# A feed-forward layer with a sine: angle and turns made by ScalarE straight from PSUM, rounding in one VectorE operation, the sine added by TensorE through a diagonal

## The chip, the cores and the metric

The kernel runs on one core of a Trainium2 chip, as one launch. The metric is the device time of that launch in microseconds (us). A core has a matrix engine (TensorE, PE in the profile, with its weight loads as PEld), a vector engine (VectorE, DVE), a scalar engine for activations (ScalarE, ACT), a general engine (GpSimd, POOL) and a queue engine (SyncE, SP). Each works through its own list of instructions in order and waits for the others by semaphores.

## The reference

Four layers, each an attention-like part and a feed-forward part, are applied to 2 x 1024 tokens of width 128 with a layer norm ahead of each. The change is in the feed-forward part of the first layer:

```python
imag = w_imag * jnp.sin(theta + hidden * 0.1)
quantum_phase = jnp.cos(theta) * w_real + jnp.sin(theta) * w_imag
return hidden + quantum_phase * imag * 0.1
...
hidden = jnp.einsum('bsd,df->bsf', x, W1) + b1
q = _quantum_transform(hidden, quantum_phases, quantum_weights_real, quantum_weights_imag)
act = jax.nn.relu(q)
return jnp.einsum('bsf,fd->bsd', act, W2) + b2
```

Width 128 goes to 512 hidden features and back. `theta`, `w_real` and `w_imag` have one value for each hidden feature, so everything that multiplies the sine is one coefficient per feature, `coef`.

## The kernel before

The program is a row of stages, one after the other on the same core; each allocates its own buffers and semaphores, and all engines meet at a barrier at its end. Nothing of a later stage is loaded ahead. The stage of the change is `l0_ffn`, whose buffers are named l0f_ in the profile. Its input is `xnT`, the normalised tokens with features on the 128 partitions and 2048 tokens along the rest; its result is added to `x`.

The work is cut into 16 items `n` = (g, c): four groups `g` of 512 tokens times four chunks `c` of 128 hidden features. For one item the kernel before does this:

- TensorE: a 128x512 matmul of `w1` and `xnT` into one of two PSUM buffers `hid` (L1014).
- ScalarE, `keep` (L932): hidden plus `b1` out of PSUM into `h`.
- VectorE, `angle`: the argument 0.1 h + theta (L973), then `turns_removed`, which takes whole turns out of it, since the sine is wanted on a bounded argument: multiply and add the constant `ROUND` (L882), subtract it again (L883), three multiply-and-subtract operations with the parts of two pi (L885), a clamp (L886).
- ScalarE, `sine` (L936), then VectorE, `combine` (L979): h + coef * sine, then ScalarE, `relu` (L943), into `a`.
- TensorE, `down` (L1007): after the four chunks of a group, 16 matmuls of 128x128, four for each chunk, into `outp`; then VectorE, `add` (L986), adds `outp` to `x`.

`h` and `y` have three buffers each, `hid` and `outp` two. A float32 matmul stands in the trace as two records, and has two weight loads. The order of work on each engine is written out by hand: VectorE does `angle(n)`, then `combine(n - 1)`, and at n = 5, 9 and 13 `add` of the group before. TensorE does `down(g - 1)` behind the matmul of item 4g + 1, but it runs ahead of the other engines, and so takes each chunk as soon as its `relu` is done. Every operation of `angle` waits for the one ahead of it to be done (`step.then_wait`), as it reads that one's result. At the stage's start VectorE works out `coef` on 128x4 tiles, and GpSimd adds the output bias to `x` (L918).

Of the kernel before, what the change touches and what calls it, by code (L numbers as in the profile page):

```python
# [5 lines left out]
ALU = mybir.AluOpType  # L6
ACT = mybir.ActivationFunctionType
# [6 lines left out]
P = 128  # L14
# [860 lines left out]
TWO_PI_PARTS = (6.28125, 0.0019350051879882812, 3.0199159819e-07)  # L875
ROUND = 1.5 * 2.0 ** 23
PI_IN = 3.1415925


def turns_removed(dve, step, y, m):  # L880

    step.then_wait(dve, dve.tensor_scalar(m, y, 0.15915494309189535, ROUND, ALU.mult, ALU.add))  # L882
    step.then_wait(dve, dve.tensor_scalar(m, m, ROUND, None, ALU.subtract))  # L883
    for part in TWO_PI_PARTS:
        step.then_wait(dve, dve.scalar_tensor_tensor(y, m, -part, y, ALU.mult, ALU.add))  # L885
    return dve.tensor_scalar(y, y, PI_IN, -PI_IN, ALU.min, ALU.max)  # L886


def l0_ffn(nc, d, x, xnT):

    F = d["f0_w1"].shape[1]
    FC = F // P
    with ExitStack() as ctx:
        sb, pb, sem = scope(nc, ctx, "l0f")
        w1, w2 = sb("w1", [P, F]), sb("w2", [P, FC, P])
        vec = sb("vec", [P, 4, FC])
        b2 = sb("b2", [P, P])
        coef, cosr, sinr, room = (sb(n, [P, FC]) for n in ("coef", "cosr", "sinr", "room"))
        h, y, m = sb("h", [P, 3, 512]), sb("y", [P, 3, 512]), sb("m", [P, 512])
        a = sb("a", [P, 2, FC, 512])  # L900
        hid = [pb(f"hid{n}", [P, 512]) for n in range(2)]
        outp = [pb(f"outp{n}", [P, 4, P]) for n in range(2)]
        w_in, bias_added = sem("w_in"), sem("bias_added")
        hid_ready, hid_kept, y_ready, sine_done = sem("hid_ready"), sem("hid_kept"), sem("y_ready"), sem("sine_done")
        q_ready, act_ready, out_ready, out_kept = sem("q_ready"), sem("act_ready"), sem("out_ready"), sem("out_kept")
        dve_step, angle_ready, trig_ready = sem("dve_step"), sem("angle_ready"), sem("trig_ready")
        items = [(g, c) for g in range(4) for c in range(FC)]
        block = ctx.enter_context(nc.Block(no_gpsimd_drain=True))

        @block.sync  # L910
        def _(sp):
            for dst, src in ((w1, d["f0_w1"]), (vec, d["f0_vec"]), (w2, d["f0_w2"]), (b2, d["f0_b2"].partition_broadcast(P))):
                sp.dma_start(dst[:], src).then_inc(w_in, 16)

        @block.gpsimd
        def _(pool):
            pool.wait_ge(w_in, 64)
            pool.tensor_tensor(x[:, :, :], x[:, :, :], b2[:, :].unsqueeze(1).broadcast_to([P, TT, P]),  # L918
                               ALU.add).then_inc(bias_added, 1)

        @block.scalar
        def _(act):
            act.wait_ge(angle_ready, 1)
            act.activation(sinr[:, :], vec[:, 1, :], ACT.Sin).then_inc(trig_ready, 1)
            act.activation(cosr[:, :], vec[:, 1, :], ACT.Sin, scale=0.5).then_inc(trig_ready, 1)

            def keep(n):
                g, c = items[n]
                act.wait_ge(hid_ready, n + 1)
                if n >= 3:  # L930
                    act.wait_ge(act_ready, n - 2)
                act.activation(h[:, n % 3, :], hid[n % 2][:, :], ACT.Identity, bias=vec[:, 0, c:c + 1]).then_inc(hid_kept, 1)  # L932

            def sine(n):
                act.wait_ge(y_ready, n + 1)
                act.activation(y[:, n % 3, :], y[:, n % 3, :], ACT.Sin).then_inc(sine_done, 1)  # L936

            def relu(n):
                g, c = items[n]
                act.wait_ge(q_ready, n + 1)  # L940
                if g >= 2:
                    act.wait_ge(out_ready, g - 1)
                act.activation(a[:, g % 2, c, :], h[:, n % 3, :], ACT.Relu).then_inc(act_ready, 1)  # L943

            keep(0)
            for n in range(len(items)):
                if n + 1 < len(items):
                    keep(n + 1)
                sine(n)
                if n >= 1:  # L950
                    relu(n - 1)
            relu(len(items) - 1)

        @block.vector
        def _(dve):
            step = Count(dve_step)
            dve.wait_ge(w_in, 64)
            turns_removed(dve, step, vec[:, 1, :], room[:, :]).then_inc(angle_ready, 1)
            dve.wait_ge(trig_ready, 2)

            step.then_wait(dve, dve.tensor_tensor(cosr[:, :], cosr[:, :], cosr[:, :], ALU.mult))
            step.then_wait(dve, dve.tensor_scalar(cosr[:, :], cosr[:, :], -2.0, 1.0, ALU.mult, ALU.add))
            step.then_wait(dve, dve.tensor_tensor(cosr[:, :], cosr[:, :], vec[:, 2, :], ALU.mult))
            step.then_wait(dve, dve.tensor_tensor(coef[:, :], sinr[:, :], vec[:, 3, :], ALU.mult))
            step.then_wait(dve, dve.tensor_tensor(coef[:, :], coef[:, :], cosr[:, :], ALU.add))
            step.then_wait(dve, dve.tensor_tensor(coef[:, :], coef[:, :], vec[:, 3, :], ALU.mult))
            step.then_wait(dve, dve.tensor_scalar(coef[:, :], coef[:, :], 0.1, None, ALU.mult))

            def angle(n):
                g, c = items[n]  # L970
                dve.wait_ge(hid_kept, n + 1)
                s = y[:, n % 3, :]
                step.then_wait(dve, dve.tensor_scalar(s, h[:, n % 3, :], 0.1, vec[:, 1, c:c + 1], ALU.mult, ALU.add))  # L973
                turns_removed(dve, step, s, m[:, :]).then_inc(y_ready, 1)

            def combine(n):
                g, c = items[n]
                dve.wait_ge(sine_done, n + 1)
                dve.scalar_tensor_tensor(h[:, n % 3, :], y[:, n % 3, :], coef[:, c:c + 1], h[:, n % 3, :],  # L979
                                         ALU.mult, ALU.add).then_inc(q_ready, 1)  # L980

            def add(g):
                dve.wait_ge(out_ready, g + 1)
                dve.wait_ge(bias_added, 1)
                s = x[:, 4 * g:4 * g + 4, :]
                dve.tensor_tensor(s, outp[g % 2][:, :, :], s, ALU.add).then_inc(out_kept, 1)  # L986

            for n in range(len(items)):
                angle(n)
                if n >= 1:  # L990
                    combine(n - 1)
                if n % FC == 1 and n > FC:
                    add(n // FC - 1)
            combine(len(items) - 1)
            add(3)

        @block.tensor
        def _(pe):
            pe.wait_ge(w_in, 64)

            def down(g):
                if g >= 2:
                    pe.wait_ge(out_kept, g - 1)
                for c in range(FC):
                    pe.wait_ge(act_ready, FC * g + c + 1)
                    for t in range(4):
                        mm = pe.matmul(outp[g % 2][:, t, :], a[:, g % 2, c, t * P:(t + 1) * P], w2[:, c, :],  # L1007
                                       start=(c == 0 and t == 0), stop=(c == FC - 1), skip_group_check=True)
                mm.then_inc(out_ready, 1)

            for n, (g, c) in enumerate(items):
                if n >= 2:
                    pe.wait_ge(hid_kept, n - 1)
                pe.matmul(hid[n % 2][:, :], w1[:, c * P:(c + 1) * P], xnT[:, g * 512:(g + 1) * 512],  # L1014
                          start=True, stop=True).then_inc(hid_ready, 1)
                if c == 1 and g >= 1:
                    down(g - 1)
            down(3)
def l1_attention(nc, d, x, xnT, ident):

# [1606 lines left out]
def program(nc, d, out, upto=99, start=0):  # L2627
    with ExitStack() as ctx:
        sb, pb, sem = scope(nc, ctx, "main")
        x = sb("x", [P, TT, P])  # L2630
        xnT = sb("xnT", [P, TOK])
        ident = sb("ident", [P, P])
# [12 lines left out]
        def layer(n, name, f, **k):  # L2645
            if start <= n < upto:
                prenorm(nc, "n" + name, x, xnT, ident, **k)
                f()

        layer(0, "0", lambda: l0_attention(nc, d, x, xnT, ident, None), rounds=2, gamma=gin[:, :])  # L2650
        layer(1, "1", lambda: l0_ffn(nc, d, x, xnT))
        layer(2, "2", lambda: l1_attention(nc, d, x, xnT, ident))

        def l1_ffn():
# [51 lines left out]
```

## Time and profile before

| | |
|---|---|
| median of 3 runs | 2371.45 us (2366.53 to 2375.58) |
| the profiled execution's own time | 2371.62 us |
| its span | 2369.9 us |
| the stage, first matmul to end of last add | 1321.58 to 1409.32 us, 87.7 us |

The profile is of one execution. The span runs from its first to its last recorded instruction. Times of day below are microseconds from the span's start. The busy share of an engine counts the instructions' own time; the granted clock (PEclk) is a share of full speed, 0.50 being 1.2 GHz and 1.00 being 2.4 GHz, averaged over a stretch.

### The profile page before, as it was taken

How to read it: one execution, taken by the hardware profiler on the slowest of the kernel's cores; microseconds unless marked ns; L12 is line 12 of the kernel's file. 1: busy time of each engine (PE TensorE's matmuls, PEld its weight loads, DVE VectorE, ACT ScalarE, POOL GpSimd, SP SyncE). 2: the span in 40 equal slices, each digit the busy share in tenths (PEclk: the TensorE clock that was granted, in tenths of full speed). 3: DMA queues.
4: the chain of work that ended last, by engine and by line, in shares of the span. 5: the costliest groups of instructions: out<-in, count | busy, mean ns of one | idle time of the engine just before them, and what ended most of it. 6: DMA issues, size and time to landing. Idle time of an engine off the chain costs nothing. (4 is left out here: it accounts for less than half of the span.)

```text
span 2369.9 us, 25752 instructions
## 1 busy us (share of the span) xinstructions
PE 1798.6 (76%) x8561; PEld 1103.2 (47%) x8561; DVE 1164.2 (49%) x2590; ACT 778.7 (33%) x1139; POOL 789.6 (33%) x618
## 2 busy tenths in 40 slices
PE   3999999999989999999997448795422853767647
PEld 1555555555555555555556234663422521222337
DVE  5434434344344442443433883345760356999814
ACT  1343334333423344333431332132101135545312
POOL 0433343333413443334331001000104301889533
PEclk8898989989899899898998667797656965899858
DMA  2101110011101100111000000000131101222051
GB/s 56 23 6 23 22 22 18 4 22 22 23 1 23 23 18 4 22 22 22 18 0 1 11 0 6 1 18 12 48 121 57 54 13 38 80 80 71 20 141 62
DMA packets 52733, 72.67 MB, mean 31 GB/s; under 512 B 10320, under 2 KB 36072, under 8 KB 52384
## 3 DMA queue, kind: packets, MB, share of 16 engines
q1 hardware_dynamic: 49744, 65.69, 10.3%
q0 software_dynamic: 2912, 6.02, 0.7%
q8 instruction: 40, 0.66, 0.1%
q14 instruction: 37, 0.30, 0.0%
HBM read 42.75 MB, written 12.15 MB: 23 GB/s over the span
## 5 line engine op out<-in xcount | busy, mean ns | idle before, releaser
L763 DVE TENSOR_REDUCE l0a_mx<-l0a_ring 128x1 fp32r<-128x128 f32 (+7 forms) x256 | 182.4, 751 | 175.7 <-PE l0a_ring L513 175.5
L771 DVE SCALAR_TENSOR_TENSOR l0a_scrap<-l0a_ring,main_ident 128x128 f32<-128x128 f32 x256 | 74.5, 291 | 348.6 <-PE l0a_ring L541 250.9
L354 POOL TENSOR_TENSOR l0a_acc<-l0a_acc,l0a_E 128x768 f32<-128x768 f32 (+2 forms) x192 | 212.5, 1132 | 69.1 <-ACT l0a_E L424 68.2
L354 POOL TENSOR_TENSOR l0a_acc<-l0a_E 128x896 f32<-128x896 f32 x32 | 66.1, 2085 | 454.2 <-ACT l0a_E L424 454.2
L540 PE MATMUL l0a_ring<-l0a_Q,l0a_K 128*128 128x512 f32 (+3 forms) x384 | 174.8, 458 | 47.7 <-ACT l0a_E L424 47.4
L424 ACT ACTIVATE l0a_E<-l0a_ring 128x1024 f32<-128x1024 f32 (+7 forms) x256 | 161.4, 650 | 130.3 <-DVE l0a_scrap L771 127.2
L2370 PE MATMUL mx_ysum<-mx_hst,main_ident 128*128 128x512 f32 x256 | 141.4, 687 | 46.1 <-POOL mx_hst L2458 40.6
L2471 POOL TENSOR_TENSOR mx_dBu<-mx_XI,mx_BB 128x1024 f32<-128x1024 f32 x64 | 137.5, 2176 | 91.9 <-DVE mx_XI L2534 91.9
L511 PE MATMUL l0a_ring<-l0a_K,l0a_Q 64*128 64x512 f32 (+3 forms) x384 | 140.5, 419 | 25.9 <-DVE l0a_mx L763 21.0
L553 PE MATMUL l0a_agg<-l0a_E,l0a_VH 128*64 128x512 f32 (+3 forms) x768 | 154.6, 510 | 0.2 <-ACT l0a_E L424 0.2
L553 PE MATMUL l0a_agg<-l0a_E,l0a_F 128*64 128x512 f32 (+3 forms) x768 | 148.5, 502 | 0.0
L541 PE MATMUL l0a_ring<-l0a_Q,l0a_K 65*128 65x512 f32 (+3 forms) x384 | 146.1, 380 | 0.0
L540 PEld LDWEIGHTS l0a_ring<-l0a_Q,l0a_K 128*128 128x128 f32 x384 | 84.0, 219 | 128.7 <-ACT l0a_E L424 102.0
L2443 ACT ACTIVATE mx_dA<-mx_DT,mx_A 128x512 f32<-128x512 f32 x128 | 88.0, 690 | 98.6 <-DVE mx_hst L2551 98.5
L2370 PEld LDWEIGHTS mx_ysum<-mx_hst,main_ident 128*128 128x128 f32 x256 | 53.6, 217 | 117.1 <-POOL mx_hst L2458 59.6
L511 PEld LDWEIGHTS l0a_ring<-l0a_K,l0a_Q 64*128 64x128 f32 x384 | 64.3, 193 | 83.4 <-DVE l0a_mx L763 60.2
L162 PE MATMUL n_turned<-main_ident,n_xn 128*128 128x128 f32 x96 | 25.8, 456 | 89.7 <-DVE n_xn L132 89.7
L491 PE MATMUL l0a_ring<-l0a_wp,main_xnT 128*128 128x256 f32 x256 | 85.5, 506 | 3.1 <-DVE l0a_mx L763 3.1
L2551 DVE TENSOR_TENSOR_SCAN mx_hst<-mx_dA,mx_hst,mx_dBu 128x512 f32<-128x512 f32 x64 | 82.1, 1283 | 7.6 <-DVE mx_hst L2551 0.5
L601 PEld LDWEIGHTS l0a_prod<-l0a_gnn,l0a_UT 128*128 128x128 f32 x512 | 77.9, 229 | 15.2 <-issue 13.0
L601 PE MATMUL l0a_prod<-l0a_gnn,l0a_UT 128*128 128x128 f32 x512 | 83.8, 317 | 0.7 <-ACT l0a_UT L451 0.7
L541 PEld LDWEIGHTS l0a_ring<-l0a_Q,l0a_K 65*128 65x128 f32 x384 | 83.0, 216 | 0.8
(467 smaller groups left out, 3613.2 us busy)
## 6 DMA issues: line engine op xcount, KB each, us to landing
mx_BB<-mx_brows SPq DMA_DIRECT2D x32, 512.0 KB, 3.6
l0a_K<-l0a_K SPq DMA_DIRECT2D x32, 256.0 KB, 3.7
l0a_Q<-l0a_Q SPq DMA_DIRECT2D x32, 256.0 KB, 4.4
me_W<-in_f_w SPq DMA_DIRECT2D x16, 256.0 KB, 9.2
l0a_wp<-in_wqkv SPq DMA_DIRECT2D x16, 192.0 KB, 2.3
moe_Wg<-in_f_wg SPq DMA_DIRECT2D x8, 256.0 KB
moe_Wu<-in_f_wu SPq DMA_DIRECT2D x8, 256.0 KB
moe_Wd<-in_f_wd SPq DMA_DIRECT2D x8, 256.0 KB
```

The costliest lines, as they stand in the source:

```text
L354: pool.tensor_tensor(dst, src, E[:, h, ecol[jt]:ecol[jt] + w], ALU.add).then_inc(acc_done, 1)
L424: act.activation(E[:, h, ecol[jt]:ecol[jt] + w], ring[h][:, 0:w], ACT.Exp).then_inc(exp_done, 1)
L491: mm = pe.matmul(ring[c][:, t * 2 * P:(t + 1) * 2 * P], xnT[:, tok:tok + P], wp[:, 2 * P:4 * P], start=True, stop=True)
L511: pe.matmul(ring[h][:, c0:c1], Q1[0:DH, h, it * P:(it + 1) * P], K1[0:DH, h, c0:c1], start=True, stop=c1 < w)
L540: pe.matmul(out, K1[:, h, keys], Q1[:, h, at], start=True, stop=False, skip_group_check=True)
L541: mm = pe.matmul(out, K2[:, h, keys], Q2[:, h, at], start=False, stop=c0 > 0, skip_group_check=True)
L553: mm = pe.matmul(agg[c][cols, lo - 512 * c:512], feats[:, jt, cols], E[:, h, at + lo:at + hi], start=(jt == 0), stop=(jt == 4 * c + 3 and ...
L601: mm = pe.matmul(prod[:, t * P:(t + 1) * P], UT[:, at:at + P], gnn[l][:, :], start=True, stop=True)
L763: dve.tensor_reduce(mx[:, h, it:it + 1], ring[h][:, 0:(it + 1) * P], AX_X, ALU.max).then_inc(max_done, 1)
L2370: mm = pe.matmul(ysum[h][:, c * 512:(c + 1) * 512], ident[:, :], hst[:, k % DEEP, c * 512:(c + 1) * 512], start=(n == 0), stop=(n == NS - ...
L2443: act.activation(dA[:, c * 512:(c + 1) * 512], DT[:, h, b * SEQ + c * 512:b * SEQ + (c + 1) * 512], ACT.Exp, scale=A[:, h, n:n + 1]).then_ ...
L2471: pool.tensor_tensor(dBu[:, k % DEEP, :], du_of(h, b), BB[:, q % 3, :], ALU.mult).then_inc(dBu_ready, 1)
```

## The change

ScalarE reads each matmul's result from PSUM twice (`angle`): once as turns, hidden/(10 * 2 pi) + `start`, into `m`, and once as the angle, 0.1 hidden + `phase`, into `y`. `phase` and `start` are worked out once on 128x4 tiles. VectorE (`reduce`) rounds `m` by one operation that adds and subtracts `ROUND`, then does the three subtractions and the clamp as before. `hidden` is not kept apart any more: TensorE adds coef * sine to the hidden values in their PSUM buffer, by a 128x512 matmul with the diagonal matrix `diag` (`add_sine`), and `relu` reads the sum from PSUM and adds `b1`. `combine` is gone. `hid` now has four buffers instead of two, each held from its first matmul until its `relu`; `y` and `m` have four each. `diag` is made by four VectorE operations. `add` on VectorE stands behind the whole of `reduce` of item 4g + 2, and `down(g - 1)` on TensorE behind `add_sine(4g + 1)` and the hidden matmul of item 4g + 4.

```diff
--- before.py
+++ after.py
@@ -886,7 +886,11 @@
     return dve.tensor_scalar(y, y, PI_IN, -PI_IN, ALU.min, ALU.max)
 
 
-def l0_ffn(nc, d, x, xnT):
+TURN = 0.15915494309189535
+HIDS, WORKS = 4, 4
+
+
+def l0_ffn(nc, d, x, xnT, ident):
 
     F = d["f0_w1"].shape[1]
     FC = F // P
@@ -896,15 +900,19 @@
         vec = sb("vec", [P, 4, FC])
         b2 = sb("b2", [P, P])
         coef, cosr, sinr, room = (sb(n, [P, FC]) for n in ("coef", "cosr", "sinr", "room"))
-        h, y, m = sb("h", [P, 3, 512]), sb("y", [P, 3, 512]), sb("m", [P, 512])
+        phase, start = sb("phase", [P, FC]), sb("start", [P, FC])
+        diag = sb("diag", [P, FC, P])
+        y, m = sb("y", [P, WORKS, 512]), sb("m", [P, WORKS, 512])
         a = sb("a", [P, 2, FC, 512])
-        hid = [pb(f"hid{n}", [P, 512]) for n in range(2)]
+        hid = [pb(f"hid{n}", [P, 512]) for n in range(HIDS)]
         outp = [pb(f"outp{n}", [P, 4, P]) for n in range(2)]
         w_in, bias_added = sem("w_in"), sem("bias_added")
...
         dve_step, angle_ready, trig_ready = sem("dve_step"), sem("angle_ready"), sem("trig_ready")
         items = [(g, c) for g in range(4) for c in range(FC)]
+        N = len(items)
         block = ctx.enter_context(nc.Block(no_gpsimd_drain=True))
 
         @block.sync
@@ -923,41 +931,61 @@
             act.wait_ge(angle_ready, 1)
             act.activation(sinr[:, :], vec[:, 1, :], ACT.Sin).then_inc(trig_ready, 1)
             act.activation(cosr[:, :], vec[:, 1, :], ACT.Sin, scale=0.5).then_inc(trig_ready, 1)
-
-            def keep(n):
+            act.wait_ge(angle_ready, 2)
+
+            def angle(n):
                 g, c = items[n]
                 act.wait_ge(hid_ready, n + 1)
-                if n >= 3:
-                    act.wait_ge(act_ready, n - 2)
-                act.activation(h[:, n % 3, :], hid[n % 2][:, :], ACT.Identity, bias=vec[:, 0, c:c + 1]).then_inc(hid_kept, 1)
+                if n >= WORKS:
+                    act.wait_ge(sum_ready, n - WORKS + 1)
+                w = n % WORKS
+                act.activation(m[:, w, :], hid[n % HIDS][:, :], ACT.Identity, bias=start[:, c:c + 1],
+                               scale=0.1 * TURN).then_inc(turns_kept, 1)
+                act.activation(y[:, w, :], hid[n % HIDS][:, :], ACT.Identity, bias=phase[:, c:c + 1],
+                               scale=0.1).then_inc(angle_kept, 1)
 
             def sine(n):
                 act.wait_ge(y_ready, n + 1)
-                act.activation(y[:, n % 3, :], y[:, n % 3, :], ACT.Sin).then_inc(sine_done, 1)
+                act.activation(y[:, n % WORKS, :], y[:, n % WORKS, :], ACT.Sin).then_inc(sine_done, 1)
 
             def relu(n):
                 g, c = items[n]
-                act.wait_ge(q_ready, n + 1)
+                act.wait_ge(sum_ready, n + 1)
                 if g >= 2:
                     act.wait_ge(out_ready, g - 1)
-                act.activation(a[:, g % 2, c, :], h[:, n % 3, :], ACT.Relu).then_inc(act_ready, 1)
-
-            keep(0)
-            for n in range(len(items)):
-                if n + 1 < len(items):
-                    keep(n + 1)
+                act.activation(a[:, g % 2, c, :], hid[n % HIDS][:, :], ACT.Relu, bias=vec[:, 0, c:c + 1]).then_inc(act_ready, 1)
+
+            angle(0)
+            angle(1)
+            for n in range(N):
                 sine(n)
+                if n + 2 < N:
+                    angle(n + 2)
                 if n >= 1:
                     relu(n - 1)
-            relu(len(items) - 1)
+            relu(N - 1)
 
         @block.vector
         def _(dve):
             step = Count(dve_step)
             dve.wait_ge(w_in, 64)
             turns_removed(dve, step, vec[:, 1, :], room[:, :]).then_inc(angle_ready, 1)
+            dve.wait_ge(angle_ready, 1)
+            step.then_wait(dve, dve.scalar_tensor_tensor(phase[:, :], vec[:, 0, :], 0.1, vec[:, 1, :], ALU.mult, ALU.add))
+            dve.tensor_scalar(start[:, :], phase[:, :], TURN, None, ALU.mult).then_inc(angle_ready, 1)
+
+            def reduce(n):
+                w = n % WORKS
+                k, s = m[:, w, :], y[:, w, :]
+                dve.wait_ge(turns_kept, n + 1)
+                step.then_wait(dve, dve.tensor_scalar(k, k, ROUND, ROUND, ALU.add, ALU.subtract))
+                dve.wait_ge(angle_kept, n + 1)
+                for part in TWO_PI_PARTS:
+                    step.then_wait(dve, dve.scalar_tensor_tensor(s, k, -part, s, ALU.mult, ALU.add))
+                dve.tensor_scalar(s, s, PI_IN, -PI_IN, ALU.min, ALU.max).then_inc(y_ready, 1)
+
+            reduce(0)
             dve.wait_ge(trig_ready, 2)
-
...
-
-            def angle(n):
-                g, c = items[n]
-                dve.wait_ge(hid_kept, n + 1)
-                s = y[:, n % 3, :]
-                step.then_wait(dve, dve.tensor_scalar(s, h[:, n % 3, :], 0.1, vec[:, 1, c:c + 1], ALU.mult, ALU.add))
-                turns_removed(dve, step, s, m[:, :]).then_inc(y_ready, 1)
-
-            def combine(n):
-                g, c = items[n]
-                dve.wait_ge(sine_done, n + 1)
-                dve.scalar_tensor_tensor(h[:, n % 3, :], y[:, n % 3, :], coef[:, c:c + 1], h[:, n % 3, :],
-                                         ALU.mult, ALU.add).then_inc(q_ready, 1)
+            for c in range(FC):
+                dve.tensor_scalar(diag[:, c, :], ident[:, :], coef[:, c:c + 1], None, ALU.mult).then_inc(coef_ready, 1)
 
             def add(g):
                 dve.wait_ge(out_ready, g + 1)
@@ -985,13 +1002,10 @@
                 s = x[:, 4 * g:4 * g + 4, :]
                 dve.tensor_tensor(s, outp[g % 2][:, :, :], s, ALU.add).then_inc(out_kept, 1)
 
-            for n in range(len(items)):
-                angle(n)
-                if n >= 1:
-                    combine(n - 1)
-                if n % FC == 1 and n > FC:
+            for n in range(1, N):
+                reduce(n)
+                if n % FC == 2 and n > FC:
                     add(n // FC - 1)
-            combine(len(items) - 1)
             add(3)
 
         @block.tensor
@@ -1008,13 +1022,30 @@
                                        start=(c == 0 and t == 0), stop=(c == FC - 1), skip_group_check=True)
                 mm.then_inc(out_ready, 1)
 
-            for n, (g, c) in enumerate(items):
-                if n >= 2:
-                    pe.wait_ge(hid_kept, n - 1)
-                pe.matmul(hid[n % 2][:, :], w1[:, c * P:(c + 1) * P], xnT[:, g * 512:(g + 1) * 512],
-                          start=True, stop=True).then_inc(hid_ready, 1)
-                if c == 1 and g >= 1:
-                    down(g - 1)
+            def hidden(n):
+                g, c = items[n]
+                if n >= HIDS:
+                    pe.wait_ge(act_ready, n - HIDS + 1)
+                pe.matmul(hid[n % HIDS][:, :], w1[:, c * P:(c + 1) * P], xnT[:, g * 512:(g + 1) * 512],
+                          start=True, stop=False, skip_group_check=True).then_inc(hid_ready, 1)
+
+            def add_sine(n):
+                g, c = items[n]
+                pe.wait_ge(sine_done, n + 1)
+                pe.wait_ge(angle_kept, n + 1)
+                if n == 0:
+                    pe.wait_ge(coef_ready, FC)
+                pe.matmul(hid[n % HIDS][:, :], diag[:, c, :], y[:, n % WORKS, :], start=False, stop=True,
+                          skip_group_check=True).then_inc(sum_ready, 1)
+
+            for n in range(3):
+                hidden(n)
+            for n in range(N):
+                add_sine(n)
+                if n + 3 < N:
+                    hidden(n + 3)
+                if n % FC == 1 and n > FC:
+                    down(n // FC - 1)
             down(3)
 def l1_attention(nc, d, x, xnT, ident):
```

The two places where the order counts follow. On VectorE, around the first `add`, items 5 to 7 before (L979 is `combine`, L973 to L886 are `angle`, L986 is `add`):

```order
L886 TENSOR_SCALAR l0f_y<-l0f_y 128x512
L979 SCALAR_TENSOR_TENSOR l0f_h<-l0f_y,l0f_coef,l0f_h 128x512
L986 TENSOR_TENSOR main_x<-l0f_outp,main_x 128x512
L973 TENSOR_SCALAR l0f_y<-l0f_h,l0f_vec 128x512
L882 TENSOR_SCALAR l0f_m<-l0f_y 128x512
L883 TENSOR_SCALAR l0f_m<-l0f_m 128x512
L885 SCALAR_TENSOR_TENSOR l0f_y<-l0f_m,l0f_y 128x512 x3
```

The same place now (L981 rounds, L984 subtracts, L985 clamps, L1003 is `add`):

```order
L981 TENSOR_SCALAR l0f_m<-l0f_m 128x512
L984 SCALAR_TENSOR_TENSOR l0f_y<-l0f_m,l0f_y 128x512 x3
L985 TENSOR_SCALAR l0f_y<-l0f_y 128x512
L1003 TENSOR_TENSOR main_x<-l0f_outp,main_x 128x512
L981 TENSOR_SCALAR l0f_m<-l0f_m 128x512
L984 SCALAR_TENSOR_TENSOR l0f_y<-l0f_m,l0f_y 128x512 x3
```

`add(0)` has gone from behind item 5's angle to behind item 6's, and `reduce(7)` stands behind it.

On TensorE, around the first `down`, before (L1014 is the hidden matmul of items 3 to 7, L1007 is `down`):

```order
L1014 MATMUL l0f_hid1<-main_xnT,l0f_w1 128x512
L1014 MATMUL l0f_hid0<-main_xnT,l0f_w1 128x512
L1014 MATMUL l0f_hid1<-main_xnT,l0f_w1 128x512
L1007 MATMUL l0f_outp0<-l0f_w2,l0f_a 128x128 x16
L1014 MATMUL l0f_hid0<-main_xnT,l0f_w1 128x512
L1014 MATMUL l0f_hid1<-main_xnT,l0f_w1 128x512
```

The same place now (L1029 is the hidden matmul of items 7, 8 and 9, L1038 is `add_sine` of items 5, 6 and 7, L1021 is `down(0)`):

```order
L1029 MATMUL l0f_hid3<-main_xnT,l0f_w1 128x512
L1038 MATMUL l0f_hid1<-l0f_y,l0f_diag 128x512
L1029 MATMUL l0f_hid0<-main_xnT,l0f_w1 128x512
L1021 MATMUL l0f_outp0<-l0f_w2,l0f_a 128x128 x16
L1038 MATMUL l0f_hid2<-l0f_y,l0f_diag 128x512
L1029 MATMUL l0f_hid1<-main_xnT,l0f_w1 128x512
L1038 MATMUL l0f_hid3<-l0f_y,l0f_diag 128x512
```

`down(0)` has moved behind the hidden matmul of item 8, which waits for `relu(4)`, and the sums of items 6 and 7 stand behind it.

## Rows read from the trace of the kernel before

**Rows 1.** The page's head, and the first row of the chain that ended last:

```profile
span 2369.9 us, 25752 instructions
...
2274.58 0.06 issue
```

**Rows 2.** Busy us of PE, PEld, DVE, ACT, POOL, granted clock, DMA share, GB/s:

```profile
1320.00:1410.00 90.00, 49.62 (x160) 31.34 (x160) 79.84 (x145) 30.46 (x50) 4.50 (x1) 0.67 0.00 1
1352.00:1354.00 2.00, 2.00 (x9) 2.00 (x10) 1.88 (x4) 0.00 (x0) 0.00 (x0) 0.50 0.00 0
1354.00:1356.00 2.00, 2.00 (x4) 0.81 (x3) 1.95 (x4) 0.25 (x1) 0.00 (x0) 0.52 0.00 0
1356.00:1366.00 10.00, 4.79 (x22) 2.61 (x20) 9.55 (x18) 4.90 (x9) 0.00 (x0) 1.00 0.00 1
1366.00:1368.00 2.00, 1.47 (x7) 1.48 (x8) 1.86 (x5) 1.16 (x2) 0.00 (x0) 0.54 0.00 0
1840.00:1880.00 40.00, 40.00 (x214) 29.16 (x213) 15.03 (x36) 9.61 (x22) 12.44 (x13) 1.00 0.07 22
2070.00:2090.00 20.00, 11.19 (x28) 4.28 (x28) 18.85 (x17) 9.61 (x14) 20.00 (x10) 0.99 0.17 56
```

**Rows 3.** Timeline of one item: start us, us, engine, line, operation [idle before <-releaser]:

```profile
1384.28 0.74 DVE L979 SCALAR_TENSOR_TENSOR l0f_h<-l0f_y,l0f_coef,l0f_h 128x512 f32<-128x512 f32 x1
1384.94 0.48 DVE L973 TENSOR_SCALAR l0f_y<-l0f_h,l0f_vec 128x512 f32<-128x512 f32 x1
1385.45 0.43 DVE L882 TENSOR_SCALAR l0f_m<-l0f_y 128x512 f32<-128x512 f32 x1
1385.91 0.43 DVE L883 TENSOR_SCALAR l0f_m<-l0f_m 128x512 f32<-128x512 f32 x1
1386.38 2.14 DVE L885 SCALAR_TENSOR_TENSOR l0f_y<-l0f_m,l0f_y 128x512 f32<-128x512 f32 x3
1388.55 0.43 DVE L886 TENSOR_SCALAR l0f_y<-l0f_y 128x512 f32<-128x512 f32 x1
1388.90 0.74 DVE L979 SCALAR_TENSOR_TENSOR l0f_h<-l0f_y,l0f_coef,l0f_h 128x512 f32<-128x512 f32 x1
1389.01 0.63 ACT L936 ACTIVATE l0f_y<-l0f_y 128x512 f32<-128x512 f32 x1 [2.55 <-DVE l0f_y L886]
```

**Rows 4.** Timeline, ScalarE and matmuls, at both levels of the clock:

```profile
1321.58 3.76 PE L1014 MATMUL l0f_hid<-main_xnT,l0f_w 128*128 128x512 f32 x4 [6.64 <-DMA l0f_b<-in_f_b]
...
1327.16 1.25 ACT L932 ACTIVATE l0f_h<-l0f_hid,l0f_vec 128x512 f32<-128x512 f32 x2
...
1334.03 2.08 PE L1014 MATMUL l0f_hid<-main_xnT,l0f_w 128*128 128x512 f32 x2 [3.04 <-ACT l0f_h L932]
...
1358.31 1.12 PE L1014 MATMUL l0f_hid<-main_xnT,l0f_w 128*128 128x512 f32 x2 [0.69 <-ACT l0f_h L932]
...
1404.82 3.78 PE L1007 MATMUL l0f_outp<-l0f_w,l0f_a 128*128 128x128 f32 x16 [2.60 <-ACT l0f_a L943]
...
1833.86 2.97 PE L1875 MATMUL e_outp<-moe_Wd,e_a 128*128 128x128 f32 x24
```

**Rows 5.** Groups by line, stage: busy us, mean ns | idle before, releaser:

```profile
L932 ACT ACTIVATE l0f_h<-l0f_hid,l0f_vec 128x512 f32<-128x512 f32 x16 | 10.8, 684 | 12.3 <-PE l0f_hid L1014 11.3
```

**Rows 6.** Timeline of the stage's ends, the adds, and a VectorE scaling:

```profile
1298.16 2.14 DVE L865 TENSOR_SCALAR l0a_Y<-l0a_Y,l0a_l0o_mv,l0a_l0o_rstd 128x128 f32<-128x128 f32 x8
...
1326.76 0.17 DVE L886 TENSOR_SCALAR l0f_vec<-l0f_vec 128x4 f32<-128x4 f32 x1
...
1355.75 0.68 DVE L986 TENSOR_TENSOR main_x<-l0f_outp,main_x 128x512 f32<-128x512 f32 x1
...
1394.18 0.68 DVE L986 TENSOR_TENSOR main_x<-l0f_outp,main_x 128x512 f32<-128x512 f32 x1
1394.78 0.48 DVE L973 TENSOR_SCALAR l0f_y<-l0f_h,l0f_vec 128x512 f32<-128x512 f32 x1
...
1408.63 0.69 DVE L986 TENSOR_TENSOR main_x<-l0f_outp,main_x 128x512 f32<-128x512 f32 x1 [3.75 <-PE l0f_outp L1007]
```

More of the change, by code:

```diff
@@ L898, in l0_ffn @@
         coef, cosr, sinr, room = (sb(n, [P, FC]) for n in ("coef", "cosr", "sinr", "room"))
-        h, y, m = sb("h", [P, 3, 512]), sb("y", [P, 3, 512]), sb("m", [P, 512])
+        phase, start = sb("phase", [P, FC]), sb("start", [P, FC])
+        diag = sb("diag", [P, FC, P])
+        y, m = sb("y", [P, WORKS, 512]), sb("m", [P, WORKS, 512])
         a = sb("a", [P, 2, FC, 512])
-        hid = [pb(f"hid{n}", [P, 512]) for n in range(2)]
+        hid = [pb(f"hid{n}", [P, 512]) for n in range(HIDS)]
         outp = [pb(f"outp{n}", [P, 4, P]) for n in range(2)]
         w_in, bias_added = sem("w_in"), sem("bias_added")
-        hid_ready, hid_kept, y_ready, sine_done = sem("hid_ready"), sem("hid_kept"), sem("y_ready"), sem("sine_done")
-        q_ready, act_ready, out_ready, out_kept = sem("q_ready"), sem("act_ready"), sem("out_ready"), sem("out_kept")
+        hid_ready, angle_kept, turns_kept, y_ready = sem("hid_ready"), sem("angle_kept"), sem("turns_kept"), sem("y_ready")
+        sine_done, sum_ready, act_ready = sem("sine_done"), sem("sum_ready"), sem("act_ready")
+        out_ready, out_kept, coef_ready = sem("out_ready"), sem("out_kept"), sem("coef_ready")
         dve_step, angle_ready, trig_ready = sem("dve_step"), sem("angle_ready"), sem("trig_ready")
         items = [(g, c) for g in range(4) for c in range(FC)]
+        N = len(items)
         block = ctx.enter_context(nc.Block(no_gpsimd_drain=True))
@@ L2650, in program @@
         layer(0, "0", lambda: l0_attention(nc, d, x, xnT, ident, None), rounds=2, gamma=gin[:, :])
-        layer(1, "1", lambda: l0_ffn(nc, d, x, xnT))
+        layer(1, "1", lambda: l0_ffn(nc, d, x, xnT, ident))
         layer(2, "2", lambda: l1_attention(nc, d, x, xnT, ident))
```

## The prediction

> **What bounds the kernel now.** I read the page's head and the chain first: the span is 2369.9 us, and the chain that ended last reaches back only to 2274.58 [rows 1]. It says nothing of the stage, which lies before it and is closed off by barriers at both ends with nothing loaded ahead; so whatever the stage gains or loses is the kernel's. Next the stage's own stretch: of 90 us VectorE is busy 79.8, TensorE 49.6, ScalarE 30.5, at a mean granted clock of 0.67 [rows 2]. The timeline of one item shows why. VectorE starts `combine` at 1384.28 and the next at 1388.90, 4.62 us an item, with no idle time noted, while ScalarE's sine waits 2.55 us for the clamp [rows 3]. With `add` a group of four takes 19.2 us: from the add at 1355.75 to that at 1394.18 lie two groups [rows 6]. VectorE bounds the stage until its end, where the last `add` waits 3.75 us for `down` [rows 6].
>
> **What the change takes from VectorE.** Out of each item go the 0.1 h + theta (1384.94 to 1385.45: 0.51), one of the two roundings (0.46) and `combine` (0.66) [rows 3]. What stays, one `reduce`: rounding 0.46, three subtractions 2.18 (1386.38 to 1388.55), clamp 0.35 until the next operation starts: **2.98 us** an item. The combined add and subtract is not in the trace; the nearest row is the clamp, also two constants on one 128x512 tile, 0.43, the same as either half of the rounding. If VectorE alone set the pace, 16 x 1.64 = 26 us would go.
>
> **What it gives ScalarE.** Three reads of PSUM instead of one, and a sine. A pair of L932 takes 1.25 us and one 0.684 [rows 4, 5], so 0.59 from start to start of them, and 0.53 for the sine (0.63 [rows 3] less the same overlap). Item: 3 x 0.59 + 0.53 = 2.3 us, under 2.98. The Trainium skill (ScalarE: Activation LUTs, Rules for kernel authors) speaks against this move: it wants additions and multiplications on VectorE, not ScalarE. The rows agree that one such operation is shorter there, 0.48 against 0.68; by that rule the 0.51 and 0.46 would stay on VectorE and cost 16 x 0.97 = 15.5 us of it. Here VectorE is the busy engine, so I do not follow it.
>
> **What it gives TensorE.** A 128x512 matmul takes 2.08 us at 1.2 GHz and 1.12 at 2.4; two in a row take 3.76 at 1.2 [rows 4], so the next starts 1.7 us after one at 1.2 and, halved, 0.86 at 2.4. Now there are two per item. A whole `down` is 32 records: 24 like ones take 2.97 at 2.4 [rows 4], so 32 take 3.87; 16 take 3.78 at 1.2, so 32 take 7.2. `down` was spread over VectorE's waits before; it now comes in one piece, behind the hidden matmul of item 4g + 4.
>
> **The new wait.** `add(g - 1)` stands on VectorE behind `reduce(4g + 2)` and waits for this `down`. Queued behind it is `reduce(4g + 3)`, and so everything of the next items: ScalarE's sine, the sum, `relu`, and TensorE's next hidden. Follow one round, from an `add`'s start, with 0.04 for each hand-over (clamp's end 1388.98 to sine 1389.01 [rows 3]):
> add 0.60 (1394.18 to 1394.78 [rows 6]); three `reduce` 8.94 and the clamp's last 0.09; hand-over and sine(4g + 5) 0.57; the two reads of `angle(4g + 7)` 1.18, which stand ahead of `relu(4g + 4)`, 0.69; hand-over and hidden(4g + 8) 0.90; `down` 3.87; hand-over 0.04. That is **16.9 us** a group at 2.4 GHz, 2.3 less than before, of which VectorE idles about 4.3.
> At 1.2 GHz another ring is the longer: two reads 1.18, `relu` 0.69, hidden 2.08 and two hand-overs 0.08 make 4.03 an item, since hidden(n + 3) waits for `relu(n - 1)` and `angle(n + 3)` for it. A group: add, one `reduce`, hand-over and sine 4.2; reads and `relu` 1.9; two rings 8.1; hidden 1.7; `down` 7.2: **23.1 us**, 3.9 more than before.
>
> **The sum at 2.4 GHz.** Setting-up ends with L886 at 1326.93 [rows 6]. Then: two small operations for `phase` and `start` 0.40 (an estimate from the 0.17 of L886 and a gap), first read and hand-overs 0.77, `reduce(0)` 2.98, seven small ones for `coef` 1.4 (they were there before, ahead of the first item), four for `diag` 1.07 (eight of 128x128 take 2.14 [rows 6]): 1333.55. Five `reduce` 14.9 and 0.09, and the round's tail from sine to `down` 7.25: first add at 1355.8, where it was 1355.75: the start gains nothing. Second add 1372.7. The third `down` has no hidden matmul ahead of it: 0.60 + 8.94 + 0.09 + sine 0.67 + sum 0.90 + `down` 3.91 = 15.1, 1387.8 (before 1394.18). The tail: 0.60 + one `reduce` 3.07 + sine 0.67 + sum 0.90 + `down` 3.91 + add 0.69 = 9.8: end 1397.6 against 1409.32. **-11.7 us.** All at 1.2 GHz: first add 1364.4 (hidden(3), behind the first sum, ends at 1337.4; reads and `relu` 1.9 to hidden(4), four rings of 4.03 to hidden(8), then 1.7 and 7.2), second 1387.5, third 1408.3 (4.2 + 1.9 + one ring 4.0 + hidden and sum 3.4 + 7.2), tail 14.0 (0.6 + 3.07 + 0.67 + 1.75 + 7.2 + 0.69): end 1422.3, **+13.0 us**.
>
> **The clock between.** In the trace it stood at 0.50 and 0.52 through 1352 to 1356 while TensorE was busy all the time, then at 1.00 for ten microseconds at 48% busy, and was back near 0.5 in 1366 to 1368 after sparse work [rows 2]. Elsewhere 56% busy held 0.99 over 20 us, and full work 1.00 [rows 2]. In the changed stage TensorE has 2 x 1.12 in 3.0 us within a group, some 70%, then `down`, then little until `reduce(4g + 3)` is through. So I expect 2.4 GHz mostly, with a fall behind some of the stalls. A hidden and a `down` at 1.2 cost 0.85 + 3.3 = 4.2 more; I charge a quarter of it four times, 4.3. Stage: -11.7 + 4.3 = **-7.4**. Against the profiled execution's own 2371.6 us that is 2364.2; the median stands 0.2 lower, so **2364.0**.
>
> **Rivals.**
> A. *The clock stays low* (slower). Every fall makes TensorE late, and its lateness passes to VectorE through `add`. All at 1.2: +13.0, about 2384. It decides from 47% of the way between the sums on (11.7 of 24.7). For it: the stage's own mean was 0.67, and each stall of VectorE empties TensorE. Against it: a low clock keeps TensorE nearly always busy (2 x 1.7 of 4.03 us, and 7.2 in one piece), and after such stretches it rose. The Trainium skill (TensorE: Matmul & The Clock Gate, HAM oscillation) has the same rule, that waits between bursts of matmuls bring the half clock back; the trace agrees at 1366. Chance 0.20, with all ends from -4 to +13.
> B. *`add` does not hold VectorE*: `down` is done when `add` comes. Then VectorE needs 4 x 2.98 + 0.6 = 12.5 a group, its last pass ends about 1380, with a tail of 6.2 at 1386.3: -23, 2348. For it only that two `outp` buffers would allow it; against it the order, `down(g - 1)` behind a hidden matmul that waits for `relu(4g)`, which is later than `reduce(4g + 2)` ends less `down`'s own time. Chance 0.08.
> C. *The change doesn't move the bound*: ScalarE's extra reads slow it under the contention of three engines on PSUM, to over 3.0 us an item. At 3.5 each of 15 passes is 0.5 longer, 7.5 in all on top of -7.4: 2371.7, no change. Nothing in the rows shows such a slowing. Chance 0.05.
> The forecast, stalls at a mostly high clock, -12 to -4, keeps 0.67.
>
> **How the numbers follow.** A measurement of this kernel can tell about 0.5%, 11.9 us, from no change. The forecast's best end, -11.7, just misses it; with the runs' scatter (4 us to either side) a tenth of its chance passes it: 0.07, and B 0.08: faster 0.15. Slower by 0.5% needs nearly the whole of A, or a further ring I have not seen: 0.05. The rest, 0.80, is within 0.5%. The range: low end the all-high sum less scatter, 2371.5 - 11.7 - 2.8 = 2357; high end A's middle, +2.5: 2374. This leaves out B and A's upper half.
>
> **What would show it.** VectorE: rounding 0.43, 2.98 from rounding to rounding within a group, and 4 to 6 us idle before the first three `add`, released by `down`; adds 17 to 19 us apart. ScalarE busy some 40 us. TensorE's clock near 0.9 in the stage, and a solid `down` of 4 to 7 us. Wrong if no wait stands before `add` (B), if the stage's clock is below 0.75 (A), or if anything outside the stage changes its length.

## The result and the profile after

The changed kernel takes 2396.47 us (median of 6 runs, 2392.51 to 2398.38), the kernel before on the same chip 2373.14 us (6 runs, 2366.53 to 2377.70): ratio 1.0095, 95% interval 1.0078 to 1.0113. It is 23 us **slower**, by 0.95%; 7.4 us faster was forecast, 2364.0. Its profiled execution took 2398.38 us with a span of 2396.7 us, 26.8 more than before.

First the changed stage, as windows of the changed kernel; the columns are those of [rows 2]. The row runs from the stage's first matmul to the end of its last `add`:

```profile
core 0: us, PE busy (x) PEld busy (x) DVE busy (x) ACT busy (x) POOL busy (x), PEclk, DMA share, GB/s
1323.40:1402.60 79.20, 55.57 (x192) 28.92 (x192) 55.72 (x103) 39.02 (x66) 4.50 (x1) 0.84 0.00 1
```

The same stretch took 87.7 us before: the stage is 8.5 us shorter. In it, VectorE from one item to the next (timeline of the changed kernel):

```profile
1337.90 0.43 DVE L985 TENSOR_SCALAR l0f_y<-l0f_y 128x512 f32<-128x512 f32 x1
1338.25 0.42 DVE L981 TENSOR_SCALAR l0f_m<-l0f_m 128x512 f32<-128x512 f32 x1
1338.70 2.15 DVE L984 SCALAR_TENSOR_TENSOR l0f_y<-l0f_m,l0f_y 128x512 f32<-128x512 f32 x3
1340.88 0.43 DVE L985 TENSOR_SCALAR l0f_y<-l0f_y 128x512 f32<-128x512 f32 x1
1341.22 0.42 DVE L981 TENSOR_SCALAR l0f_m<-l0f_m 128x512 f32<-128x512 f32 x1
```

One rounding, three subtractions and a clamp: 2.97 us from rounding to rounding, where an item took 4.62 [rows 3]. Then the four `add`, with the first and the last `down` (same timeline):

```profile
1354.49 3.73 PE L1021 MATMUL l0f_outp<-l0f_w,l0f_a 128*128 128x128 f32 x32
1358.26 0.69 DVE L1003 TENSOR_TENSOR main_x<-l0f_outp,main_x 128x512 f32<-128x512 f32 x1 [5.06 <-PE l0f_outp L1021]
1375.23 0.69 DVE L1003 TENSOR_TENSOR main_x<-l0f_outp,main_x 128x512 f32<-128x512 f32 x1 [4.38 <-PE l0f_outp L1021]
1391.14 0.69 DVE L1003 TENSOR_TENSOR main_x<-l0f_outp,main_x 128x512 f32<-128x512 f32 x1 [3.33 <-PE l0f_outp L1021]
1396.91 4.95 PE L1021 MATMUL l0f_outp<-l0f_w,l0f_a 128*128 128x128 f32 x32
1401.90 0.69 DVE L1003 TENSOR_TENSOR main_x<-l0f_outp,main_x 128x512 f32<-128x512 f32 x1 [7.09 <-PE l0f_outp L1021]
```

`down` is one solid piece, and VectorE stands still ahead of each `add` until it is done: 19.9 us in four waits. The first three, 12.8 us, are the forecast ring, nearly to the number; the fourth, 7.09 us, is the tail behind the last item. So the loss lies elsewhere. I cut the whole span at the first operation of each layer norm from the stage's own on:

| from norm to norm, us | before | after | difference |
|---|---|---|---|
| start to the norm ahead of `l0_ffn` | 1304.2 | 1306.8 | +2.6 |
| that norm and `l0_ffn` | 106.0 | 96.7 | -9.3 |
| next norm and `l1_attention` | 95.1 | 127.7 | **+32.6** |
| next norm and `l1_ffn` | 104.2 | 103.3 | -0.9 |
| next norm and the attention after it | 82.0 | 83.2 | +1.2 |
| the rest | 678.4 | 678.9 | +0.5 |

The loss is in a stage that the change doesn't touch: its instructions are the same, 368 matmul records in both. First before, in windows (the last row is norm and stage together):

```profile
1410.20:1441.20 31.00, 16.65 (x64) 9.04 (x64) 18.43 (x61) 5.87 (x8) 6.43 (x3) 0.72 0.04 10
1441.20:1465.10 23.90, 20.57 (x74) 11.78 (x75) 14.75 (x24) 1.97 (x2) 0.00 (x0) 0.50 0.00 1
1465.10:1505.30 40.20, 37.63 (x232) 28.23 (x230) 6.47 (x21) 14.01 (x27) 4.67 (x16) 1.00 0.00 1
1410.20:1505.30 95.10, 74.84 (x368) 49.05 (x368) 39.65 (x105) 21.85 (x36) 11.11 (x19) 0.78 0.01 4
```

and the same pieces of the changed kernel:

```profile
1403.50:1437.00 33.50, 18.08 (x66) 9.44 (x66) 19.75 (x63) 5.84 (x8) 6.42 (x3) 0.75 0.04 10
1437.00:1458.40 21.40, 18.98 (x72) 10.89 (x71) 13.41 (x22) 1.01 (x1) 0.00 (x0) 0.50 0.00 0
1458.50:1531.20 72.70, 70.25 (x233) 52.84 (x232) 6.48 (x21) 14.99 (x27) 4.67 (x16) 0.50 0.00 0
1403.46:1531.19 127.73, 107.41 (x368) 73.17 (x368) 39.66 (x105) 21.87 (x36) 11.10 (x19) 0.56 0.01 3
```

The first two pieces together are as long in both, 54.9 and 55.0 us. In the third, 232 matmul records take 37.6 us busy at 1.00 before and 70.3 at 0.50 after. TensorE is the bound there, so the stage grows by as much. The costliest groups of that stage, before:

```profile
L1161 PE MATMUL l1a_agg<-l1a_V,l1a_E 128*128 128x65 f32 x144 | 16.6, 273 | 0.0
L1143 PE MATMUL l1a_ring<-l1a_qa,l1a_ka 65*128 65x512 f32 x24 | 12.5, 632 | 0.0
```

and after:

```profile
L1192 PE MATMUL l1a_agg<-l1a_V,l1a_E 128*128 128x65 f32 x144 | 31.4, 413 | 0.0
L1174 PE MATMUL l1a_ring<-l1a_qa,l1a_ka 65*128 65x512 f32 x24 | 22.5, 1074 | 0.0
```

The two groups alone give 24.8 us. In both kernels the clock falls at the start of the second piece (0.50 in it). What differs is whether it comes back up where the last piece starts. In this stage the row maxima are turned by 32 small bf16 matmuls (L1128 and L1129 before, L1159 and L1160 after), and behind them comes the long row of float32 ones. Before, 2 us at a time:

```profile
1460.00:1462.00 2.00, 1.47 (x15) 1.47 (x16) 0.66 (x5) 0.00 (x0) 0.00 (x0) 0.50 0.00 0
1462.00:1464.00 2.00, 2.00 (x20) 1.81 (x18) 0.00 (x0) 1.01 (x1) 0.00 (x0) 0.50 0.00 0
1464.00:1466.00 2.00, 2.00 (x5) 0.97 (x5) 0.00 (x0) 1.84 (x2) 0.00 (x0) 0.71 0.00 0
```

After:

```profile
1454.00:1456.00 2.00, 0.99 (x10) 0.99 (x11) 1.14 (x5) 0.00 (x0) 0.00 (x0) 0.50 0.00 0
1456.00:1458.00 2.00, 2.00 (x22) 2.00 (x20) 0.00 (x0) 1.01 (x1) 0.00 (x0) 0.50 0.00 0
1458.00:1460.00 2.00, 2.00 (x8) 1.13 (x6) 0.00 (x0) 1.36 (x2) 0.00 (x0) 0.50 0.00 0
1460.00:1462.00 2.00, 2.00 (x3) 0.67 (x2) 0.00 (x0) 0.93 (x1) 0.00 (x0) 0.50 0.00 0
1572.00:1574.00 2.00, 2.00 (x3) 0.34 (x1) 0.00 (x0) 1.21 (x1) 0.00 (x0) 0.62 0.00 0
```

The instructions of the burst and of what follows are the same. Before, the clock goes up within 2 us behind it and stays up; after, it does not, and it isn't up until 1573, 136 us after 1437.0, although TensorE was busy for 70.3 of the 72.7 us of the long row. The last 42 of these 136 us lie in the next stage, in which the clock is low before, too, from 1506 to 1550.

### The profile page after: what moved, and what is told of

Read it like the earlier page. It is cut to its first block and busy times, and to the rows that moved or that the text cites. A ratio compares the mean times of both kernels' runs of the same rounds, so it can differ in the third digit from the quotient of the medians.

```text
span 2396.7 us, 25821 instructions
## 1 busy us (share of the span) xinstructions
PE 1837.2 (77%) x8593; PEld 1123.1 (47%) x8593; DVE 1140.1 (48%) x2548; ACT 787.8 (33%) x1155; POOL 789.8 (33%) x618
```

## The experiments

**Theory 1**: whether the clock rises in `l1_attention` hangs on when the work falls there, and the change moved it 6.7 us earlier; a shift without the change should do the same, and more work for TensorE ahead of the long row should bring the rise back. **Theory 2**: the changed stage itself leaves TensorE in a lasting low clock. **Theory 3**: the change costs something of its own there.

### Matmuls that bring the clock up

Two more 128-high matmuls, ahead of the burst in `l1_attention`, in both kernels. Their results are used by nothing; all else is computed as it was.

```diff
+            for k in range(2):
+                pe.matmul(agg[3][:, :], ident[:, :], xnT[:, 0:512], start=True, stop=True)
             for b in range(2):
                 pe.wait_ge(mparts, b + 1)
```

> The changed kernel with two extra 128x512 matmuls (results unused) put into the next stage, l1_attention, where TensorE waits for VectorE ahead of the row-maximum matmuls. Theory 1 (the loss is the clock: in that stage TensorE stood at 1.2 GHz from 1437 us to the end, where before it rose at 1465, and only because the short burst of matmuls fell differently in time): dense full-height work right there raises the clock, l1_attention with its norm falls from 128 us to about 96, and the total from 2396.5 to about 2365, some 8 us under the kernel before. Theory 2 (the changed layer leaves something lasting behind, a hold on the clock that later work can't lift): l1_attention stays near 128 us and the total near 2398.

> The kernel before with the same two extra matmuls in l1_attention. Both theories: the clock rises there anyway, so within 3 us of 2373, up to 2 us more for the extra work, or a little less if the clock now rises earlier. It is the base for the first kernel: the difference of the two is what the change does to its own layer, forecast -7 to -9 us.

Measured: the changed kernel with them 2370.61 us (5 runs, 2369.81 to 2376.93), 0.9962 of before [0.9948, 0.9976]. The kernel before with them 2381.95 (10 runs, 2372.56 to 2383.22), 1.0008 [0.9996, 1.0020]. Before on this chip: 2378.76. The windows of the changed kernel with them:

```profile
1436.30:1456.80 20.50, 19.79 (x51) 9.47 (x52) 13.37 (x22) 0.00 (x0) 0.00 (x0) 0.50 0.00 0
1456.80:1494.30 37.50, 36.33 (x233) 26.84 (x231) 3.69 (x16) 15.82 (x27) 4.67 (x16) 1.00 0.00 1
```

and, in its timeline, the two matmuls (four records):

```profile
1452.36 3.73 PE L1157 MATMUL l1a_agg<-main_xnT,main_ident 128*128 128x512 f32 x4
```

The clock is up within the burst, at 1456.8, and the row that took 70.3 us busy takes 36.3. From norm to norm this stage is 98.5 us, `l0_ffn` 96.7; with the same matmuls the kernel before has 97.1 and 106.4. So between two kernels whose clock rises at the same place, the change is worth 11.3 us by the medians, where 7 to 9 was expected, and 9.7 by the stage; against the plain kernel before it is 8.2 us. The edit's own price is 2 to 3 us (ratio 1.0008, medians 2381.95 against 2378.76); the interval reaches 4.8. Theory 2 would have wanted the clock to stay low here, and theory 3 an `l1_attention` some 30 us longer than in the kernel before: neither is so.

The two matmuls also fill the 1.7 us for which TensorE waits there and put the burst off by about as much, so this delay might have done it alone. The traces speak against that. Two more traces of this edit are of the kernels further down, and in three of the four the clock rises while the two matmuls still run, ahead of the burst: at 1462.2 in the kernel before, with the burst from 1462.6 on, at 1440.8 (1441.1) and at 1438.6 (1439.0). The rise comes 2.9 to 4.4 us after the first of them starts, in all four.

### A delay behind the stage, with and without the change

Small VectorE operations (about 0.72 us each) that write `m` over itself, behind the stage's last `add`: two, five, one or four of them (`m[:, 0, :]` in the changed kernel). They put off all that follows; `m` is used no more there, so nothing computed differs.

```diff
             add(3)
+            for k in range(2):
+                step.then_wait(dve, dve.tensor_tensor(m[:, :], m[:, :], m[:, :], ALU.min))
```

> The kernel before with two idle-like VectorE operations (0.7 us each) behind the layer's last add, so that l1_attention begins 1.4 us later and nothing else differs. Theory 1: when the work comes decides, so the time may jump by up to +30 us to about 2403 though only 1.4 us were added; if this shift happens to leave the clock's rise in place, 2374.5. Theory 2: 2374.5, never more.

> The changed kernel with the same 1.4 us of delay behind its last add. Theory 1: may fall by 30 us to about 2367, or stay at 2398 if the shift leaves the clock down. Theory 2: 2398.

> The kernel before with five 0.7 us operations behind the layer's last add, 3.6 us of delay. If it is the lateness of l1_attention as such that keeps the clock down (any delay of 1.4 us or more), it stays near 2409, l1_attention with its norm at 127 to 128 us. If it is how the work falls against the moments at which the clock is set, a further delay can bring the rise back: l1_attention near 95 us, total near 2379 + 3.6 = 2382.

> The changed kernel with 0.7 us of delay behind its last add. By the first theory one of the shifts between 0 and 3.6 us finds the moment at which the clock rises in l1_attention: there its stage is 95 to 98 us in place of 128 and the total near 2372. I give this one a chance of one in three. A lasting hold on the clock: 128 us whatever the shift.

> The changed kernel with 2.9 us of delay. As for the 0.7 us: 95 to 98 us and a total near 2374 if the moment fits, 128 us and 2405 if not; a chance of one in two, as 0 and 1.4 us did not fit.

| kernel | time, us | ratio | `l0_ffn` | `l1_attention`, profiled |
|---|---|---|---|---|
| before + 2 | 2408.96 (4 runs) | 1.0124 [1.0107, 1.0141] | 107.3 | 127.6 |
| before + 5 | 3 runs 2407.0 to 2410.4, 7 runs 2374.7 to 2384.3 | 1.0030 [1.0002, 1.0059] | 110.2 | 127.9 |
| changed + 1 | 2402.11 (1 run) | | 100.1 | 127.7 |
| changed + 2 | 2404.49 (4 runs) | 1.0099 [1.0082, 1.0117] | 97.4 | 127.5 |
| changed + 4 | 2369.80 (1 run) | | 99.6 | 97.7 |

The ratio of before + 5 is of a mixture of both kinds of run and tells nothing by itself. The kernel before with two of them, 1.4 us of delay, is 30 us slower, in all four runs, and without anything of the change. Its windows, the long row and then norm and stage:

```profile
1467.00:1539.00 72.00, 69.59 (x232) 52.34 (x230) 6.46 (x20) 14.41 (x27) 4.72 (x16) 0.50 0.00 0
1411.42:1539.02 127.60, 107.46 (x368) 73.31 (x368) 39.66 (x105) 21.88 (x36) 11.15 (x19) 0.54 0.01 3
```

They read like those of the changed kernel. The profiled run of the changed kernel with four of them has no loss:

```profile
1405.30:1503.00 97.70, 77.09 (x368) 50.32 (x368) 39.63 (x104) 21.86 (x36) 11.11 (x19) 0.76 0.01 4
```

This settles theory 1 against 2 and 3: the loss comes without the change, and the change comes without the loss. It does not follow the shift alone, though: I had taken the length of the shift to decide, and before + 5 came out both ways within one batch. The stage has two lengths, 95 to 99 and 127.5 to 128 us, and nothing in between in any trace.

### The same kernels again

> The changed kernel with 2.9 us of delay once more, now timed in rounds. One look gave 2369.8 us with the clock up in l1_attention. If the shift fixes the outcome, all its times lie near 2371; if it only changes the odds, some lie near 2402, as the kernel before with 3.6 us of delay gave times near 2378 and near 2409.

Ten runs of changed + 4: 2362.87, 2367.11, 2373.48 and 2375.07, and six from 2400.51 to 2407.65. The profiled one is a short one, with 95.4 us in the stage. So four operations don't cure it; the single run had been luck. No long run of this kernel was profiled. The kernel before, in the 19 runs of this batch, lay 13 times between 2371.45 and 2382.68 and **6 times between 2408.42 and 2411.32**. In its 33 runs of the other batches, beside the changed kernel and in the experiments above, it never rose over 2382.45. No long run of the unedited kernel before was profiled either; that these six are the same loss is read from their length, 30 us more. The loss is a chance that the kernels without the two matmuls have, in very different measure, and not a fixed cost.

The traces show more of what goes with the outcome. Take the time from the fall of the clock in this stage to the start of the burst. The mean clock of a 2 us slice gives the fall: 0.81 in the first line is 1.24 us at 1.00 and the rest at 0.50, so 1441.24. Before, then the changed kernel, each with its burst's first matmul:

```profile
1440.00:1442.00 2.00, 0.20 (x2) 0.06 (x1) 1.76 (x3) 0.00 (x0) 0.00 (x0) 0.81 0.00 0
1460.53 0.27 PE L1128 MATMUL l1a_ring<-l1a_identb,l1a_mh 128*1 128x128 bf16 x1 [1.72 <-DVE l1a_ml L1203]
...
1436.00:1438.00 2.00, 0.58 (x3) 0.39 (x3) 1.98 (x4) 0.00 (x0) 0.00 (x0) 0.75 0.01 4
1455.01 0.26 PE L1159 MATMUL l1a_ring<-l1a_identb,l1a_mh 128*1 128x128 bf16 x1 [1.73 <-DVE l1a_ml L1234]
```

That is 19.3 us where the clock rises and 18.0 where it does not. In the nine traces without the two matmuls, the five long ones have 18.0 (changed, changed + 1, before + 5), 18.3 (before + 2) and 18.5 us (changed + 2); the four short ones have 17.8 (changed + 4), 19.2 (changed + 4 again), 19.3 (before) and 19.4 us (the later `add` below). So the outcome goes with where the burst falls against the clock's own steps, and that differed by 1.4 us between two executions of one kernel. This is read from nine traces after the fact, with 17.8 and 18.0 close together, and no run tested it.

### `add` one item later

In the changed kernel VectorE stands at `add` for 19.9 us, 12.8 of them in the forecast ring. Here `add` stands behind `reduce(4g + 3)` instead of `reduce(4g + 2)`, with the two matmuls of the first experiment and without; then also with six `hid` buffers for four.

```diff
-                if n % FC == 2 and n > FC:
+                if n % FC == 3 and n > FC:
                     add(n // FC - 1)
...
-HIDS, WORKS = 4, 4
+HIDS, WORKS = 6, 4
```

> The changed kernel with the two extra matmuls in l1_attention, and add of a group one item later on VectorE (behind reduce of item 4g+3). If VectorE's wait for down, three times 3 to 5 us, is on the path, as the prediction had it, the layer loses some 9 us, to about 70 us, and the total is near 2361, 0.7% under the kernel before. If the loop of the two reads, relu and hidden matmul holds instead, under 3 us go.

> The changed kernel with the two extra matmuls, add one item later, and six hid buffers instead of four, so that hidden(n+3) waits for relu(n-3) and not relu(n-1). If the ring of two reads, relu and hidden still holds some passes over the 2.98 us of reduce, 1 to 3 us more go, total 2354; if VectorE alone holds them, no difference from 2356.

> The changed kernel with add one item later and no extra matmuls. The layer is some 11 us shorter, as in the run with both. If the rise of the clock in l1_attention hangs on the moment alone, this is open: 97 us there and a total near 2356, or 128 us and near 2387; a chance of one in three for the first. Either way the two extra matmuls are worth the difference, 0 or 30 us.

With the matmuls: 2356.26 us (4 runs, 2354.69 to 2357.61), 0.9922 [0.9906, 0.9939]. Windows of the changed stage, and of norm and `l1_attention`:

```profile
1320.20:1388.30 68.10, 50.41 (x192) 27.10 (x192) 55.58 (x103) 39.05 (x66) 4.50 (x1) 0.89 0.00 1
1389.20:1486.70 97.50, 78.58 (x372) 51.03 (x372) 39.62 (x104) 21.73 (x36) 11.11 (x19) 0.76 0.01 4
```

and in its waits of VectorE:

```profile
DVE main_x L1003 <- PE l0f_outp L1021: 8.9, 3, 4.9
```

VectorE's busy time is the same, the wait is 11.0 us shorter and the stage 11.1, where 9 was expected: `add` waiting for `down` was on the path. Of the 8.9 us left, 4.85 are the tail. Six `hid` buffers bring the wait to 5.6 us and the norm and stage from 85.5 to 82.4 us, so waiting for `relu` had still held some items, but the time, 2355.60 (4 runs, ratio 0.9887 [0.9808, 0.9966]), can't be told from that with four. Without the two matmuls the later `add` gives 2350.82 to 2359.35 in eight runs of ten and 2383.25 and 2385.04 in two: ratio 0.9908 [0.9858, 0.9958], which takes in all ten. Its eight shorter runs are as short as those with the matmuls, but it still falls back at times, by their length: neither of the two was profiled. The version to keep is the later `add` with the two matmuls: 20 us faster than the kernel before on its chip (2356.26 against 2376.32). Of the 23 runs of the four kernels with these matmuls none is a long one. For the changed kernel itself that is 5 of 5 short where 6 of 6 were long; for the others it proves less, since without the matmuls 46 of 52 (before) and 8 of 10 (later `add`) were short as well.

## Why the prediction was wrong

- **The step that failed** is the first paragraph's "so whatever the stage gains or loses is the kernel's". Barriers keep work from crossing, but they pass on the time at which the next stage starts, and its clock depended on how its work then fell. The later stages did not keep their length: +32.6 us in `l1_attention` against -9.3 here, since its long row of matmuls took 70.3 us busy at 0.50 for 37.6 at 1.00. The prediction listed "if anything outside the stage changes its length" as what would make it wrong, and gave it no chance and no price.
- **Rival A** was the clock staying low *in the changed stage*. That did not happen: 0.84 in it, forecast near 0.9. The mechanism was right, its place wrong. Every stage bound by TensorE behind the change should have been looked at, with the price of staying low: before, the long row is 37.6 us busy at 1.00 and all of it could double.
- **VectorE 2.98 us an item**: 2.97. **ScalarE** busy some 40 us: 39.0.
- **The new wait**: 5.06, 4.38 and 3.33 us where about 4.3 was forecast; `add` to `add` 17.0 and 15.9 where 16.9 and 15.1 were. `down` 3.73 us for 3.87. The tail's wait was 7.09. Rival B is out, as a wait stands before each `add`, and so is C, as an item kept 2.97 us.
- **The clock charge of 4.3**: the stage gained 8.5 where -11.7 + 4.3 = -7.4 was forecast, so by difference it was about 3.2. (A quarter of 4.2, four times, is 4.2 and not 4.3.) The last `down` took 4.95 us, partly at the low clock, which stood at 0.50 from 1396.0 to 1399.4.
- **The sum** would have been about right with the clock as it was behind the stage: with the matmuls in both kernels it is 2381.95 to 2370.61, -11.3, and -8.2 against the kernel before without them, where -7.4 was forecast.

What is shown: the loss is TensorE's clock in `l1_attention`, the change is a gain where this clock is secured, and a shift of the kernel before brings the same loss. What stays open: what decides between the two outcomes in a single run. Neither the length of a shift nor the order of work tells it, since four kernels showed both by their times (before, before + 5, changed + 4 and the later `add` without matmuls). The time from the clock's fall to the burst goes with the outcome in all nine traces, but was not tested, and that the changed kernel had six long runs of six while others are mixed is not explained. Nor is it shown what it is in the two matmuls that raises the clock: their 128 rows, their length, or that they leave TensorE no pause.

The Trainium skill (TensorE: Matmul & The Clock Gate, What's actually happening) says that the clock's monitor runs on its own, is not reset by a kernel's start, and makes the same kernel differ from run to run. No trace shows the monitor itself. That the same kernel differs, the traces and runs agree with: the two profiled executions of changed + 4 have 17.8 and 19.2 us from the clock's fall to the burst, its ten times are of two kinds, and the price is some 30 us of 2400.

## What to carry to other kernels

A stage bound by TensorE has two lengths, and which one it gets can be decided by work that lies ahead of it: look at the granted clock stage by stage, and price the other length for each of them, before and after a change. When a change behaves as forecast in its own stage and the whole does not, cut the span at marks that both kernels have, and repeat the runs, as a single run of a kernel with two outcomes proves nothing. Where a long row of matmuls starts from a low clock, two more matmuls ahead of it, at 2 to 3 us, saved about 30 here.

## What the hardware showed

- At 0.50 of the clock TensorE was busy 70.3 of 72.7 us with 65-high and 128-high float32 matmuls, and the clock did not rise; at 1.00 the same work, 37.6 of 40.2 us, held it. Both outcomes came with the same instructions and nearly the same busy share.
- 1.4 us of VectorE work that nothing uses, at the end of the stage ahead, cost 30 us in four runs of four. Two 128x512 matmuls with all 128 rows, 3.4 to 3.73 us, had the clock up 2.9 to 4.4 us after their start in each of the four traces that have them.
- A `TENSOR_SCALAR` with an added and a subtracted constant on 128x512 takes 0.42 us, one that clamps between two constants 0.43; so rounding by a large constant costs one operation.
